# The first layer's products of values and probabilities, one 64-column tile per head and a whole chunk at a time

## The reference

```python
def _mha(q_in, k_in, v_in, wq, bq, wk, bk, wv, bv, wo, bo, padding_mask, causal):
    q = (q_in @ wq + bq).reshape(Bq, Sq, H, DK).transpose(0, 2, 1, 3)   # H = 16, DK = 64
    ...
    scores = jnp.einsum('bhqd,bhkd->bhqk', q, k)
    ...
    attn = jax.nn.softmax(scores / math.sqrt(DK), axis=-1)
    out = jnp.einsum('bhqk,bhkd->bhqd', attn, v)          # the product that the change touches
    out = out.transpose(0, 2, 1, 3).reshape(Bq, Sq, H * DV)
    return out @ wo + bo
```

## Time and profile before

| what | value |
|---|---|
| time, median of 3 runs | 2759.67 us (2757.86 to 2768.1) |
| span of the profiled execution | 2759.5 us |
| PE busy | 2370.4 us (86%), x11287 |
| PEld busy | 1640.2 us (59%) |
| DVE busy | 1495.8 us (54%) |
| ACT busy | 1174.9 us (43%) |
| POOL busy | 330.8 us (12%) |
| mean granted TensorE clock | 0.893 |

### The profile page before, as it was taken

The page is one execution under the profiler, slowest core; times in us unless marked ns, Lnnn a source line. Parts: engine busy times, 40 slices in busy tenths (PEclk is TensorE's granted clock), DMA queues, the critical chain, the costliest instruction groups (busy, mean ns, idle before and its releaser), DMA issues.

```text
span 2759.5 us, 37661 instructions
## 1 busy us (share of the span) xinstructions
PE 2370.4 (86%) x11287; PEld 1640.2 (59%) x11287; DVE 1495.8 (54%) x3988; ACT 1174.9 (43%) x4009; POOL 330.8 (12%) x342
## 2 busy tenths in 40 slices
PE   6888988898898989898889988898889888975898
PEld 3554655566565656565556656565556656553596
DVE  4544666466755666466645575566646675233212
ACT  4543635273544545273525444463527353210221
POOL 0002011201111011201211011201120120112000
PEclk9999999899998999899989999999989999556555
DMA  5000000000000000000000000000000000000001
GB/s 149 1 1 13 1 1 1 14 1 1 1 1 14 1 1 1 14 1 1 1 6 10 1 1 1 14 1 1 1 5 1 1 1 1 0 1 0 0 0 30
DMA packets 24440, 20.41 MB, mean 7 GB/s; under 512 B 1685, under 2 KB 22043, under 8 KB 24219
## 3 DMA queue, kind: packets, MB, share of 16 engines
q1 hardware_dynamic: 24218, 17.72, 2.2%
HBM read 15.62 MB, written 2.10 MB: 6 GB/s over the span
## 4 chain that ended last, share of the span: by engine, by line
issue 70%; PE 13%; POOL 10%; DVE 4%; ACT 3%; SPq 0%; POOLq 0%; DMA 0%; DVEq 0%
POOL kx L573 4%; POOL rstd L550 3%; PE ps L948 2%; PE ps L944 2%; POOL s_probsT L578 2%; PE ps L653 2%; POOL main_residual L563 1%; PE ps L794 1%; PE ps L661 1%; ACT probs L986 1%; PE ps L696 1%; ACT s_probs L986 1%; PE ps L787 1%; PE ps L961 1%; POOL pool_scratch L544 1%
## 5 line engine op out<-in xcount | busy, mean ns | idle before, releaser
L986 ACT ACTIVATE probs<-ps,neg_max 128x128 f32<-128x128 f32 x1024 | 362.7, 367 | 407.5 <-DVE neg_max L1147 400.8
L986 ACT ACTIVATE s_probs<-ps,s_max 128x128 f32<-128x128 f32 x768 | 219.6, 369 | 242.0 <-DVE s_max L1147 241.8
L696 PE MATMUL ps<-keys,queries 128*128 128x256 f32 x1024 | 275.1, 391 | 28.8 <-ACT queries L980 28.8
L719 PE MATMUL ps<-probsT,values 128*128 128x256 f32 x1024 | 271.9, 388 | 3.7 <-ACT headsT L1020 2.7
L1147 DVE TENSOR_REDUCE neg_max<-ps 128x4 f32<-128x512 f32 x256 | 176.7, 690 | 147.0 <-PE ps L699 145.7
L696 PEld LDWEIGHTS ps<-keys,queries 128*128 128x128 f32 x1024 | 183.2, 191 | 117.7 <-issue 50.5
L1147 DVE TENSOR_REDUCE s_max<-ps 128x4 f32<-128x512 f32 x192 | 132.6, 691 | 218.0 <-PE ps L794 215.7
L794 PE MATMUL ps<-kx,qT 32*128 32x512 f32 (+1 forms) x384 | 238.0, 702 | 10.8 <-POOL kx L573 10.8
L1154 DVE BATCH_NORM_STATS2 stats<-ps 128x6 f32<-128x128 f32 x352 | 78.3, 285 | 298.7 <-PE ps L661 295.0
L550 POOL TENSOR_TENSOR rstd<-var_eps,minus_half 128x4 f32<-128x4 f32 x88 | 90.4, 1027 | 1217.7 <-DVE var_eps L1160 1216.9
L719 PEld LDWEIGHTS ps<-probsT,values 128*128 128x128 f32 x1024 | 175.5, 191 | 61.8 <-issue 14.7
(11 more groups left out here) (209 smaller groups left out, 4172.5 us busy)
## 6 DMA issues: line engine op xcount, KB each, us to landing
x_in<-in_x SPq DMA_DIRECT2D x8, 256.0 KB, 2.9
c_in<-in_ctx SPq DMA_DIRECT2D x8, 256.0 KB, 3.2
skip_in<-in_mask_BxS_ik SPq DMA_DIRECT2D x8, 256.0 KB, 3.3
out<-x_all SPq DMA_DIRECT2D x8, 256.0 KB, 2.3
valid_in<-in_mask_BxS_bf SPq DMA_DIRECT2D x8, 64.0 KB, 3.2
w_qkv_sa<-in_L_xattn_sa_wq SPq DMA_DIRECT2D x1, 512.0 KB
w_qkv_sa<-in_L_xattn_sa_wk SPq DMA_DIRECT2D x1, 512.0 KB
w_qkv_sa<-in_L_xattn_sa_wv SPq DMA_DIRECT2D x1, 512.0 KB
```

Of the source, the lines that this page charges most:

```text
L696: mm(bank(MAIN, item)[:, n * 256:n * 256 + 256], queries[:, c % 2, at], keys[:, c % 2, :, at], start=(n == 0), stop=False, skip_group_chec ...
L719: last = mm(bank(MAIN, item)[:, n * 256:n * 256 + 256], values[:, c // 4, b0 + n, (c % 4) * 128:(c % 4) * 128 + 128], probsT[:, u % 2, n * ...
L986: last = A(dst[:, u % dst.shape[1], h * 128:h * 128 + 128], bank(st, (tag, "s", u))[:, h * 128:h * 128 + 128], ACT.Exp, bias=src_max[:, u ...
```

## The change

The item `o` now stands for a chunk (`c`) and not for a unit. It is placed at odd s from 5 on, so that it comes when both units of its chunk have been transposed; the attention has one more step index (up to 19), and the list as a whole 116 steps and not 131. `probsT` has 4 buffers.

The product is now made per sequence and per head: the stationary operand is the 64 columns of one head's values, the moving one the 128 columns of that head's probabilities, and the result goes to the 64 partitions of that head (`64 * h`) of bank 3. A chunk is 8 matmuls (4 sequences x 2 heads), each with two passes, where it was 4. Only wanted products are made, and they lie in the bank as in `headsT`. So one copy of 128 partitions x 512 columns empties the bank, on ACT for even chunks and on DVE for odd ones.

```diff
     def attention(tag):
-        for s in range(UNITS + 3):
+        for s in range(UNITS + 4):
...
-            third = [(tag, "o", s - 3)] if s >= 3 else []
+            third = [(tag, "o", (s - 4) // 2)] if s >= 4 and s % 2 else []
...
+PT = 4
...
-        probsT = sb("probsT", [128, 2, 512])
+        probsT = sb("probsT", [128, PT, 512])
...
             def outputs(i, item):
-                tag, _, u = item
-                c, b0 = u // 2, 2 * (u % 2)
-                first_use = [(tag, "v", c // 4, b) for b in range(G)] if u % (UNITS // 2) == 0 else []
-                before_filling(i, item, (tag, "t", u), *first_use)
-                for n in range(2):
-                    last = mm(bank(MAIN, item)[:, n * 256:n * 256 + 256],
-                              values[:, c // 4, b0 + n, (c % 4) * 128:(c % 4) * 128 + 128],
-                              probsT[:, u % 2, n * 256:n * 256 + 256], start=True, stop=True)
+                tag, _, c = item
+                first_use = [(tag, "v", c // 4, b) for b in range(G)] if c % 4 == 0 else []
+                before_filling(i, item, (tag, "t", 2 * c), (tag, "t", 2 * c + 1), *first_use)
+                for b in range(G):
+                    u, n = 2 * c + b // 2, b % 2
+                    for h in range(2):
+                        at = (c % 4) * 128 + 64 * h
+                        last = mm(bank(MAIN, item)[64 * h:64 * h + 64, b * T:b * T + T], values[:, c // 4, b, at:at + 64],
+                                  probsT[:, u % PT, (2 * n + h) * 128:(2 * n + h) * 128 + 128], start=True, stop=True)
                 last.then_inc(filled[MAIN], 1)
...
-                            wait_filled(act, i, MAIN, item)
-                            for h in range(2):
-                                dst, src = head_of(item, h)
-                                last = A(dst, src, ACT.Copy)
-                            last.then_inc(emptied[MAIN, "A"], 1)
+                            take(i, MAIN, item, headsT[:, item[2], :], ACT.Copy)
...
-                            wait_filled(dve, i, MAIN, item)
-                            for h in range(2):
-                                dst, src = head_of(item, h)
-                                last = V.tensor_copy(dst, src)
-                            last.then_inc(emptied[MAIN, "D"], 1)
+                            take(i, MAIN, item, lambda s: V.tensor_copy(headsT[:, item[2], :], s))
```

More of the change, by code:

```diff
@@ L754, in main @@
                                 t = "sa" if tag == "ln1" else "ca"
-                                before_filling(i, item, *[(t, "o", u) for u in range(UNITS)])
+                                before_filling(i, item, *[(t, "o", c) for c in range(C0)])
                                 sums(MAIN, tag, lambda b: [(token(headsT[:, c, :], b), w_o[t][:, c, :]) for c in range(C0)]
@@ L1016, in main @@
                         elif kind == "o":
-                            wait_filled(act, i, MAIN, item)
-                            for h in range(2):
-                                dst, src = head_of(item, h)
-                                last = A(dst, src, ACT.Copy)
-                            last.then_inc(emptied[MAIN, "A"], 1)
+                            take(i, MAIN, item, headsT[:, item[2], :], ACT.Copy)
                         elif kind == "t":
-                            take(i, MAIN, item, probsT[:, item[2] % 2, :], ACT.Copy)
+                            take(i, MAIN, item, probsT[:, item[2] % PT, :], ACT.Copy)
                     yield
@@ L1241, in main @@
                         elif kind == "t":
-                            take(i, MAIN, item, lambda s: V.tensor_copy(probsT[:, item[2] % 2, :], s))
+                            take(i, MAIN, item, lambda s: V.tensor_copy(probsT[:, item[2] % PT, :], s))
                         elif kind == "scale":
```

5 lines of the change are left out of this document (removed).

## The result

| | before | after |
|---|---|---|
| time, median of 4 runs | 2763.05 us (2757.86 to 2768.1) | 2796.78 us (2781.85 to 2803.52) |
| span of the profiled execution | 2759.5 us | 2801.8 us |
| mean granted TensorE clock | 0.893 | 0.864 |

The ratio after to before is 1.012, with a 95% interval from 1.0088 to 1.0151. The kernel got slower, by more than the 0.5% that can be told from no change. The forecast was 2746 us, so it had the wrong sign.

The account below looks back on a forecast made before the run. PE was taken to bound the kernel, busy 86% of the span and full where 59% of the products stand. Sum: 2759.5 - 11 (PE) - 5 (copies) + 3 (order) = 2746.5, said as 2746 us; 8 in 10 from 2707 to 2797.

Parts of the forecast that it names:

- 83 ns per pass: Changed product on PE: heads overlap, but each load hides only beside the pass just ahead; 21.25 us per loop pass.
- lower bound of 59: Changed product on PE: only weight loads left, one after the other, 59 ns each; 15.1 us per loop pass.
- full overlap: Rival for the changed product on PE: both heads' tiles overlap, only loads left, 59 ns; 2712 us, chance 0.25.
- the test that I named: Time of line 715's 16 passes to the next group: 1.33 us means 83 ns, 0.95 full overlap, 1.75 none.
- The change of form: Entering and leaving 64-column tiles on PE: 0.340 us per chunk, 0.143 where shared; 4.46 us per loop pass.
- Net on PE: PE per loop pass: 21.25 + 4.46 - 27.65 = -1.9 us; -8.1 with 59 ns passes.
- How much reaches the end: Share of PE's net reaching kernel time: 0.8, over seven passes factor 5.6, so -11 us (-45 to +67).
- The copies: Fewer, larger copies on DVE and ACT: counted -5 us at the end (0 to -15).
- The order: Later product and 75 side steps over 116 main steps, changed neighbours taken as neutral: together +3 us (0 to +8).
- its slower rival: Changed product on PE: no overlap, 109 ns passes, change of form bought with nothing; 2784 us, chance 0.26.
- Rival 4: PE gets faster but the side chain takes the time, filler missing; about 2755 us, no change, chance 0.08.
- Wrong on the sign if passes of line 715 follow each other by over 91 ns: Condition on the changed product: break-even at 91 ns per pass, above which the forecast's sign would be wrong.

Follow-up runs that it names:

- e5_k_between: Changed kernel with empty step slots kept and the keys' projection moved from the first to the third slot of even s; 2682.14 us, 0.9705 of before.
- e10_k_between_wide: e5_k_between with 128-column weights (both heads) in each product of the chunk, so no tile form or overlap; 2735.64 us, 0.9902 of before.
- e2_wide_new_order: Changed kernel with 128-column weights in each of its 8 products per chunk, so no tile form or overlap; 2865.09 us, 1.0371 of before.
- e1_tiles_old_order: Kernel before, its order and 131 steps kept, with each unit's product in two 64-column tiles and one copy; 2753.38 us, 0.9965 of before.
- e4_old_fewer_steps: Kernel before with products of even step indices moved into the transposes' step, 117 main steps, same main order; 2815.83 us, 1.0199 of before.
- e6_streams: Changed kernel with each small-attention product moving up to 108 columns, not 9 or 17, same result and order; 2738.37 us, 0.9905 of before.
- e7_old_streams: Kernel before with the same wider small products as e6_streams, as control; 2759.28 us, 0.9986 of before.
- e12_padded_streams: Changed kernel with its empty step slots kept (131 steps) and the wider small products of e6_streams; 2760.74 us, 0.9993 of before.

## Why the prediction was wrong

**The cost of the passes: right mechanism, wrong choice among the cases.** I took 83 ns per pass, since the earlier trace rows show no load pulled past a waiting pass. The trace after shows 55 ns, below even the lower bound of 59 that the earlier trace rows gave. It is the case that I called full overlap: the test that I named, 0.95 us for 16 passes against 1.33 and 1.75, came out at 1.02 with the leaving in it. The rule that a weight load overlaps a matmul in flight only where the row group differs (the Trainium skill, TensorE: Matmul & The Clock Gate, The mechanism) does not hold for these two tiles: they share all 128 rows, and each of the 16 loads takes 133 to 137 ns while a pair of passes needs 109. The rule that different tiles can load and multiply in parallel (the Trainium skill, TensorEngine Tiling (Array Packing), Key Properties) fits the 55 ns.

**The change of form: right.** At full clock, away from L789, a chunk in tiles takes 1.22 us beside what its neighbours need. Eight pairs at 109 ns are 0.87 of it, so the form costs 0.35 us; the forecast had 0.34. It lies in four places: the matmul in front lasts 93 ns more, the first pair 51 (160 and not 109), the last pair 100 (209), and the first pass behind 104 (320 and not 216 for L690). Behind L789, whose own form costs some 0.19 us in either kernel, the extra is 0.15 (forecast 0.143). With 11 and 5 chunks of a pass that is 4.6 us, against 4.46. The table has +3.5 under "form", as its rule counts some of this elsewhere.

**Net on PE: better than forecast, by the cost of a pass alone.** 16 x 0.873 + 4.6 - 27.65 = -9.1 us per pass where I had -1.9, and -8.1 for full overlap (the table's "work" and "form" make -10.6). Over seven passes -9.1 is -64 us. Had all else stayed and all of it reached the end, the kernel would have stood at about 2696 us. That e5_k_between stands at 2682 is no proof of it, as the moved projection is worth 20 us by itself.

**How much reaches the end: the share was not the failure.** I counted 0.8 of the net, as PE is full in 59% of the places. Between e10_k_between_wide and e5_k_between, 12 chunks of a pass go from 1.79 to 1.22 us and the 4 behind the small scores from 1.98 to 1.22, together 9.9 us. 7.6 of these reach the end, 0.77. (Of the table's 11.5 it is 0.66.)

**The copies.** The copies to `headsT` lost 63 us on DVE (107.5 to 44.3) and 57 on ACT (97.0 to 39.8), at 692 and 621 ns each, all eight groups together; for seven passes that is 55 and 50, as forecast (at 688 and 609 ns). The engines' busy time fell by 56 and 52. Nothing of it is to be seen at the end: the waits of PE rose and did not fall. The 5 us counted for it are not shown.

**The order: here it failed.** The step reads: "The 75 side steps now spread over 116 main steps, so their neighbours change; I take that as neutral. Together +3 us (0 to +8)." What the runs show in its place: the new order with the old 128-column weights (e2_wide_new_order) costs 103 us: 12.0 us of clock, 1.9 of waits and 1.0 of longer work per pass. With tiles it costs 43 us (e1_tiles_old_order to the changed kernel), though e1 pays for twice the changes of form. So the step that I counted with 3 us is worth 43 to 103. The whole change has +10.7 us of clock and +6.0 of waits per pass, 117 us in all, and the order accounts for most of the clock but not for all of it: the tiles in the old order lose 3.9 us of clock per pass (e1), and the waits rise by 2.9 there, by 1.9 with the order alone. e4_old_fewer_steps loses 2% with the old product, again by the order. That the low clock is a cause of the loss and not a sign of it is shown by e6_streams, which alters only the columns moved and gains 58 us, while the control e7_old_streams gains none. The earlier trace rows had PEclk at 1.00 in three of four stretches, and I carried that over to the new order without a word, as if the clock belonged to the kernel and not to what stands in a row on PE. The forecast had room for a failed overlap, and its slower rival was that; the slowdown came with full overlap, by a mechanism that no rival had. (Rival 4 had the missing filler, but as lost gain, with no clock in it.) "Wrong on the sign if passes of line 715 follow each other by over 91 ns" is refuted: they follow by 55, and the sign was still wrong.

**What stays open.** How the 42 us of waits (7 x 6.0) split over the places, and between the order and a PE that is done sooner: they stay in e6_streams and e12_padded_streams, and fall by 4.2 us per pass with the keys' projection in between. Which of the falls of the clock costs how much, since I moved whole families of steps. And why the changed kernel's four runs lie 22 us apart (2781.85 at a clock of 0.869, 2803.52 at 0.864, 2795.99 at 0.863): the time roughly follows the clock there too, but no run shows what makes the clock differ between executions of one program.

## What to carry to other kernels

Before an edit takes passes out of a full PE, look at what stands next to each other when they are gone: here groups that issue much and stream little, side by side, cost more by the clock than the passes had cost. Read PEclk per stretch, before and after; a busy PE is not a streaming one. If the filler must go, put other wide matmuls (here the keys' projection) into its place, and look for that place in the order of every pass, not in the number of steps.

## What the runs showed of the hardware

- Two float32 tiles of 64 columns that share all rows run at once: pairs start 7 ns apart and follow by 109 ns, with 64-column weight loads of 133 to 137 ns hidden.
- Going into that form and out of it costs 0.35 us together: 93 ns on the matmul in front, 51 on the first pair, 100 on the last, 104 on the first pass behind (after, at full clock).
- Under a 128-column weight load, 108 moving columns cost nearly the same as 9: eight passes take 0.87 us (901.11 to 901.98, e6_streams) and not 0.81 (936.65 to 937.46, after).
- The granted clock fell from 2.4 to 1.2 GHz in a stretch in which PE is busy 97%, with no pause over 0.58 us in the timeline from 927.9 to the fall at 941.70. At the same place of the order it did not fall when the small products moved 108 columns and not 9, with a pause of 0.49 us (e6_streams).
- The same program runs at different mean clocks, and its time goes with them: 35.7 us between 0.874 and 0.887 (e1_tiles_old_order).
